# Router values in PSUM, one-column norms by partition scalars, and another engine order in both routers of an MoE-attention-MoE block

## The reference

```python
x = L0_attn_x                                        # 2048 tokens x 512
x = x + 0.5 * ffn(layernorm(x), router_w, w1, w2, w3)   # 8 experts, top 2
x = x + attention(layernorm(x), wq, wk, wv, wo)         # 16 query heads, 4 kv heads, rope, causal
x = x + 0.5 * ffn(layernorm(x), router_w, w1, w2, w3)   # the same weights

def ffn(x, ...):
    logits = x @ router_w.T                          # 8 columns
    topk_vals, topk_idx = top_k(logits, 2)
    w = softmax(topk_vals)
    out = sum_k w_k * (silu(x @ w1[e_k]) * (x @ w2[e_k])) @ w3[e_k]
```

## Time and profile before

| | |
|---|---|
| median of 3 runs | 1417.6 us (1414.39 to 1419.07) |
| profiled execution | 1419.23 us, its span 1417.9 |
| PE busy | 1220.3 us (86%) |
| DVE busy | 917.7 us (65%) |
| ACT busy | 662.2 us (47%) |
| POOL busy | 549.6 us (39%) |
| mean granted TensorE clock | 0.951 of full speed |

### The profile page before, as it was taken

One profiled execution on the slowest core, in us unless ns is written; L12 is line 12 of the kernel. 1 busy time (PEld: TensorE's weight loads), 2 busy tenths in 40 slices (PEclk: granted clock), 3 DMA queues, 4 the chain that ended last, 5 costly groups with the idle time before them and its releaser, 6 DMA issues.

```text
span 1417.9 us, 22075 instructions
## 1 busy us (share of the span) xinstructions
PE 1220.3 (86%) x7484; PEld 784.6 (55%) x7484; DVE 917.7 (65%) x2072; ACT 662.2 (47%) x1313; POOL 549.6 (39%) x458
## 2 busy tenths in 40 slices
PE   4279999948988999999989999999999538998884
PEld 3268888727776554454445455454433226766663
DVE  7777777668996565576676675767700785665653
ACT  2525545515455454454365554555566323444442
POOL 5535544323210110013353454445647443444442
PEclk8589999979999999999999999999999859999998
DMA  9713333256541022041013003013000343555544
GB/s 340 280 53 105 112 108 109 82 161 101 88 85 32 2 62 31 17 105 31 32 60 61 2 2 119 30 62 61 1 2 1 129 178 68 89 90 91 93 87 65
DMA packets 56891, 114.42 MB, mean 81 GB/s; under 512 B 7664, under 2 KB 17136, under 8 KB 56752
## 3 DMA queue, kind: packets, MB, share of 16 engines
q0 software_dynamic: 26112, 68.17, 22.0%
q1 hardware_dynamic: 30672, 44.85, 9.5%
HBM read 79.71 MB, written 33.55 MB: 80 GB/s over the span
## 4 chain that ended last, share of the span: by engine, by line
PE 58%; DMA 17%; DVE 16%; issue 4%; ACT 4%; SPq 1%; POOL 0%; POOLq 0%; DVEq 0%; ACTq 0%
DMA out<-Y,DI 12%; PE bank L1448 9%; PE bank L1460 9%; PE bank L752 9%; PE bank L907 8%; PE bank L1473 5%; PE bank L775 4%; PE bank L1510 3%; DVE PM L920 3%; DMA XA<-y 2%; DVE bank L922 2%; PE bank L734 1%; ACT P L1552 1%; PE bank L365 1%; PE bank L1490 1%
## 5 line engine op out<-in xcount | busy, mean ns | idle before, releaser
L1552 ACT ACTIVATE P<-bank 128x512 f32<-128x512 f32 (+3 forms) x640 | 305.5, 536 | 296.5 <-PE bank L1448 292.8
L920 DVE TENSOR_REDUCE PM<-bank 128x1 f32<-128x512 f32 x384 | 252.6, 685 | 99.2 <-PE bank L907 98.0
L1448 PE MATMUL bank<-Qs,Ks 98*128 98x512 f32 (+3 forms) x640 | 247.9, 412 | 7.9 <-ACT P L1552 6.3
L907 PE MATMUL bank<-Ks,Qs 96*128 96x512 f32 (+3 forms) x640 | 238.4, 391 | 9.6 <-DVE PM L920 5.0
L1448 PEld LDWEIGHTS bank<-Qs,Ks 98*128 98x128 f32 x640 | 117.3, 190 | 149.8 <-issue 84.7
L1606 POOL TENSOR_TENSOR CH<-CH,P 128x512 f32<-128x512 f32 x128 | 160.2, 1285 | 70.2 <-ACT P L1552 69.3
L922 DVE CUSTOM_DVE_ANT_0 bank<-bank,KB 128x128 f32<-128x128 f32 (+3 forms) x256 | 124.6, 496 | 57.4 <-PE bank L907 56.6
L1591 POOL TENSOR_SCALAR_AFFINE_SELECT P<-P 128x512 f32<-128x512 f32 x64 | 40.8, 638 | 308.3 <-ACT P L1552 308.3
L907 PEld LDWEIGHTS bank<-Ks,Qs 96*128 96x128 f32 x640 | 121.4, 190 | 64.0 <-DVE PM L920 32.6
L1460 PE MATMUL bank<-P,V 128*32 128x512 f32 (+3 forms) x1280 | 150.8, 542 | 0.2 <-POOL P L1591 0.2
L863 DVE TENSOR_TENSOR DL<-W,DH 128x512 fp32r<-128x512 f32 x152 | 98.3, 688 | 46.7 <-ACT DH L824 36.2
(11 more groups left out here) (176 smaller groups left out, 1936.9 us busy)
## 6 DMA issues: line engine op xcount, KB each, us to landing
xn<-XN SPq DMA_DIRECT2D x8, 1024.0 KB, 6.0
WR<-L_ffn_w POOLq DMA_DIRECT2D x16, 512.0 KB, 13.2
XO<-y POOLq DMA_DIRECT2D x8, 1024.0 KB, 9.5
WR<-L_ffn_w SPq DMA_DIRECT2D x16, 512.0 KB, 7.9
XA<-y POOLq DMA_DIRECT2D x24, 256.0 KB, 4.2
W<-L_ffn_w POOLq DMA_DIRECT2D x8, 512.0 KB, 24.2
XA<-L_attn_x SPq DMA_DIRECT2D x16, 256.0 KB, 3.5
XO<-L_attn_x SPq DMA_DIRECT2D x4, 1024.0 KB, 7.8
```

The costliest lines, as they stand in the source:

```text
L907: pe.matmul(bk(g, bank)[:, 0:n], g.Qs[b][0:96, G % 4 * 4 + h, c * P:c * P + P], g.Ks[0:96, G % 4, k * BQ:k * BQ + n], start=True, stop=Tru ...
L920: dve.tensor_reduce(dst, bk(g, bank)[:, 0:n], AX.X, ALU.max).then_inc(s(f"free{bank}"), 1)
L1448: pe.matmul(bk(g, i % 3)[:, o:BQ], g.Ks[0:98, G % 4, k * P:k * P + P], g.Qs[G // 4][0:98, G % 4 * 4 + j, o:BQ], start=True, stop=True).the ...
L1552: act.activation(a.P4[buffer_of(n)][:, j, o:BQ], bk(g, i % 3)[:, o:BQ], ACT.Exp, scale=scale).then_inc(s("exp"), 1)
```

## The change

It does five things. (1) Most intermediate values of `dve_route` are put into banks 6 and 7 (`route_banks`), so that an instruction has at most one input tensor in SBUF; a few copies are added for it (`M1`, a second half of `OH`, `tok`). (2) The Newton step of a single column takes its factors as partition scalars and has one instruction fewer (router 1's last quarter, and the 16 norms of the projection, L1119). (3) Router 0 turns two quarters ahead: the order of PE and of the banks is `first_order`, eight tiles of `xT` are held, the logits have a tile of their own, DVE handles the logits of quarter q-2 inside quarter q, and ACT makes one cast before its last four turns. (4) The tail of the plan has three of the steps `split1` before the norms and one behind each norm, the eighth behind the last turn, and the casts and subtractions behind the router are gone. (5) `TK` is made first from the slots, `DW` and `DI` behind it, and POOL waits for `TK` before it gathers and for `DI` before it writes.

The waits between the instructions are left out here:

```diff
 def router_memory(f, area, small, nx):
-    R.xT = area(f"xT{f}", [P, 4, D])
+    R.xT = area(f"xT{f}", [P, R.nt, D])          # R.nt = 4 * nx
+    R.lg = R.xT[:, 0, 0:P] if f else small("lg", [P, P])[:]
...
+def route_banks(g):
+    ps = Box()
+    a, b = bk(g, 6), bk(g, 7)
+    ps.OH = a[:, 0:256].rearrange("p (k i e) -> p k i e", k=2, e=NE)
+    ps.HF = a[:, 256:320].rearrange("p (h n) -> p h n", h=2)
+    ps.HI = a[:, 320:384].bitcast(I32).rearrange("p (h n) -> p h n", h=2)
+    ps.WV = a[:, 384:416].rearrange("p (h n) -> p h n", h=2)
+    ps.tok = a[:, 416:448]
+    ps.IF = a[:, 448:480].rearrange("p (k i) -> p k i", k=2)
+    ps.SF = a[:, 480:512]
+    ps.we, ps.M1, ps.tl, ps.en, ps.EF = ...      # bank 7
...
+def dve_newton_of_one(g, var, sd, y, t):
+    dve, dv = g.nc.vector, g.dv
+    dve.reciprocal(y, sd).then_inc(dv.sem, 1)
+    dve.tensor_scalar(t, y, y, var, ALU.mult, ALU.mult).then_inc(dv.sem, 1)
+    dve.tensor_scalar(t, t, -0.5, 1.5, ALU.mult, ALU.add).then_inc(dv.sem, 1)
+    dve.tensor_scalar(y, y, t, None, ALU.mult).then_inc(dv.sem, 1)
...
+def first_order():
+    def turns(q):
+        return [("turn", 0, 4 * q + c) for c in range(4)]
+    order = turns(0) + turns(1)
+    for q in range(4):
+        order += [("logits", 0, q), ("best", 0, q)] + (turns(q + 2) if q < 2 else [])
+    return order
...
 def act_first(g):
     act.wait_ge(s("xn0"), NT)
-    for e in range(4):
+    act_high(g, 0, 0)
+    for i in range(NT - 4, NT):
+        act_turn(g, R, i)
+    for e in range(1, 4):
         act_high(g, 0, e)
...
 def dve_first(g):
+        dve_variance(g, R, 0, 4, q)
+        if q >= 2:
+            dve_logits(g, R, q - 2)
+        dve_solve(g, R, 0, 4, q)
+        dve_room(g, R, q)
+        for c in range(4):
+            dve_scale(g, R, q, x4, c)
+        if q >= 2:
+            dve_best(g, R, q - 2)
+    for q in range(2, 4):
+        dve_logits(g, R, q)
+        dve_best(g, R, q)
...
 def dve_route(g, f, R, low_in_between):
-    dve.tensor_tensor(r.wd[:, 0, :], M8[:, :, 1], M8[:, :, 0], ALU.subtract).then_inc(rt.sem, 1)
+    dve.tensor_scalar(ps.M1, M8[:, :, 1], 1.0, None, ALU.mult).then_inc(rt.sem, 1)
+    dve.tensor_tensor(r.wd[:, 0, :], ps.M1, M8[:, :, 0], ALU.subtract).then_inc(rt.sem, 1)
-    dve.tensor_copy(r.IF[:], I8[:, :, 0:2].rearrange("p i k -> p k i")).then_inc(rt.sem, 1)
+    dve.tensor_scalar(ps.IF, I8[:, :, 0:2].rearrange("p i k -> p k i"), 1.0, None, ALU.mult).then_inc(rt.sem, 1)
+    # ps.OH <- iota, ps.IF (256 columns); r.OH[:, 1] <- iota, ps.IF (128 columns); r.A <- ps.OH[0], r.OH[1]
-    dve.tensor_tensor(r.A[:], r.OH[:, 0, :, :], r.OH[:, 1, :, :], ALU.add).then_inc(rt.sem, 1)
+    dve.tensor_tensor(r.A[:], ps.OH[:, 0, :, :], r.OH[:, 1], ALU.add).then_inc(rt.sem, 1)
+    dve.tensor_scalar(ps.tok, K[:, C_TOK:C_TOK + 2 * NT], 1.0, None, ALU.mult)
...
     for k in range(2):
-        dve.tensor_tensor(r.OH[:, k], r.SL[:], r.OH[:, k], ALU.mult).then_inc(rt.sem, 1)
+        dve.tensor_tensor(r.OH[:, k], r.SL[:], ps.OH[:, k], ALU.mult).then_inc(rt.sem, 1)
...
-    dve.tensor_copy(r.TF[:], ps[:, 0:NJ])
-    dve.tensor_copy(r.DW[:], ps[:, NJ:2 * NJ])
+    # TD, then TI and TK straight from the bank; DW and DI behind TK
...
 def pool_experts(g, f, before_adding):
-    pool.wait_ge(s(f"route{f}"), g.routed[f]["DI"])
+    pool.wait_ge(s(f"route{f}"), g.routed[f]["TK"])
...
+        if j == 1:
+            pool.wait_ge(s(f"route{f}"), g.routed[f]["DI"])
...
 def attend_plan(g):
-    plan += [("weigh", len(TILES) - 1), ("out", 15), ("up1", 4), ("tsum", 15), ("even", 15)]
+    plan += [("weigh", len(TILES) - 1), ("out", 15), ("up1", 4), ("split1", 0), ("split1", 1), ("split1", 2), ("tsum", 15), ("even", 15)]
     for c in range(6):
...
-            plan.append(("split1", c))
-    plan += [("logits", 3), ("best", 3), ("store", 3)]
+            plan.append(("split1", 3 + c))
+    plan += [("split1", 7), ("logits", 3), ("best", 3), ("store", 3)]
...
 def build(nc, d, out):
-        for e in range(4, NE):
-            act_high(g, 1, e)
-        for e in range(4, NE - 1):
-            pool_low(g, 1, e)
```

More of the change, by code:

```diff
@@ L273, in dve_solve @@
         dv.up()
-    var, sd, y, t = (sm[:, j, c0:c1] for j in range(4))
     dve.wait_ge(dv.sem, dv.n)
-    dve.tensor_scalar(var, R.mv[:, c0:c1, 1], 1e-5, None, ALU.add).then_inc(s(f"var{R.f}"), 1)
-    dve.wait_ge(s(f"sd{R.f}"), k + 1)
-    dve_newton(g, var, sd, y, t)
+    dve.tensor_scalar(sm[:, 0, c0:c1], R.mv[:, c0:c1, 1], 1e-5, None, ALU.add).then_inc(s(f"var{R.f}"), 1)
+def dve_solve(g, R, c0, c1, k):
+    g.nc.vector.wait_ge(g.s(f"sd{R.f}"), k + 1)
+    newton = dve_newton_of_one if c1 == c0 + 1 else dve_newton
+    newton(g, *(R.sm[:, j, c0:c1] for j in range(4)))
 def dve_newton(g, var, sd, y, t):
@@ L347, in act_turn @@
     act.wait_ge(s(f"full{bank}"), use + 1)
-    if i >= 4:
-        b0, u0 = g.ring.where[("best", R.f, i // 4 - 1)]
+    if i >= R.nt:
+        b0, u0 = g.ring.where[("best" if R.f else "logits", R.f, (i - R.nt) // 4)]
         act.wait_ge(s(f"full{b0}"), u0 + 1)
-    act.copy(R.xT[:, i % 4, :], bk(g, bank)).then_inc(s(f"free{bank}"), 1)
+    act.copy(R.xT[:, i % R.nt, :], bk(g, bank)).then_inc(s(f"free{bank}"), 1)
 def pe_logits(g, R, q):
@@ L373, in dve_logits @@
     dve.wait_ge(s(f"full{bank}"), use + 1)
-    dve.tensor_copy(R.xT[:, 0, 0:P], bk(g, bank)[:, 0:P]).then_inc(s(f"free{bank}"), 1)
+    dve.tensor_copy(R.lg, bk(g, bank)[:, 0:P]).then_inc(s(f"free{bank}"), 1)
 def pe_best(g, R, q):
@@ L395, in dve_best @@
     ins.then_inc(s(f"free{bank}"), 1)
-def first_plan(g):
[L402 to L406, removed]
+def first_order():
[5 more added lines that the diff above has]
+    return order
+def first_plan(g):
+    for key in first_order():
+        g.ring.take(key)
 def sp_first(g):
@@ L439, in act_first @@
     s, act, R = g.s, g.nc.scalar, g.R0
-    for q in range(5):
-        if q < 4:
-            act_sqrt(g, R, 0, 4, q)
+    for q in range(4):
+        act_sqrt(g, R, 0, 4, q)
         if q:
@@ L446, in act_first @@
     act.wait_ge(s("xn0"), NT)
-    for e in range(4):
+    act_high(g, 0, 0)
+    for i in range(NT - 4, NT):
+        act_turn(g, R, i)
+    for e in range(1, 4):
         act_high(g, 0, e)
 def pe_first(g):
-    for q in range(4):
-        for i in range(4 * q, 4 * q + 4):
+    for kind, _, i in first_order():
+        if kind == "turn":
             pe_turn(g, g.R0, i)
-        pe_logits(g, g.R0, q)
-        pe_best(g, g.R0, q)
+        elif kind == "logits":
+            pe_logits(g, g.R0, i)
+        else:
+            pe_best(g, g.R0, i)
 def dve_first(g):
     s, dve, R = g.s, g.nc.vector, g.R0
[L461 to L476, removed]
+    for q in range(4):
+        x4 = g.X[:, 4 * q:4 * q + 4, :]
+        for c in range(4):
+            if q == 0:
+                dve.wait_ge(s(f"x0_{c}"), 16)
+            elif c == 0:
+                dve.wait_ge(s(f"x{q}"), 16)
+            dve_stats(g, R, x4, c)
+        dve_variance(g, R, 0, 4, q)
[3 more added lines that the diff above has]
+        dve_room(g, R, q)
+        for c in range(4):
+            dve_scale(g, R, q, x4, c)
[4 more added lines that the diff above has]
+        dve_best(g, R, q)
 ORDER = (tuple(range(NE)), (4, 5, 6, 7, 0, 1, 2, 3))
@@ L635, in dve_route @@
     else:
[L636 removed]
+        dve.tensor_scalar(r.TD[:], sl[:, 2 * NJ:3 * NJ], g.Kc[:, C_PAD + 1:C_PAD + 2], g.Kc[:, C_PAD:C_PAD + 1],
+                          ALU.mult, ALU.add)
+        dve.tensor_copy(r.TK[:], sl[:, 0:NJ]).then_inc(rt.sem, 1)
     out["TK"] = rt.up()
[L638 removed]
+    dve.wait_ge(rt.sem, rt.n)
+    dve.tensor_copy(r.DW[:], sl[:, NJ:2 * NJ])
+    dve.tensor_tensor(r.DI[:], r.TD[:], sl[:, 0:NJ], ALU.add).then_inc(rt.sem, 1)
     out["DI"] = rt.up()
@@ L643, in act_route @@
 def act_route(g, f):
-    s, act, r = g.s, g.nc.scalar, g.r[f]
+    s, act = g.s, g.nc.scalar
     act.wait_ge(s(f"route{f}"), g.routed[f]["wd"])
-    act.activation(r.wd[:, 1, :], r.wd[:, 0, :], ACT.Exp).then_inc(s(f"we{f}"), 1)
+    act.activation(g.r[f].wd[:, 1, :], g.r[f].wd[:, 0, :], ACT.Exp).then_inc(s(f"we{f}"), 1)
 def pe_route(g, f):
@@ L1623, in pool_attend @@
                            accum_op=ALU.add).then_inc(s("xoy"), 16)
-        elif step[0] == "split1":
+        elif step[0] == "split1" and step[1] < NE - 1:
             pool_low(g, 1, step[1])
@@ L1682, in dve_attend @@
         elif kind == "solve":
+            dve_variance(g, g.R1, 0, 4, step[1])
             dve_solve(g, g.R1, 0, 4, step[1])
```

104 lines of the change are left out of this document (50 added, 54 removed).

## The result

| | before | after |
|---|---|---|
| median | 1418.34 us (1414.39 to 1423.05, 4 runs) | 1381.27 us (1377.62 to 1382.4, 4 runs) |
| ratio, 95% interval | | 0.9733 (0.9698 to 0.9768) |
| span of the profiled execution | 1417.9 us | 1381.1 us |
| mean granted TensorE clock | 0.951 | 0.958 |
| DVE busy | 917.7 us | 884.9 us |

What follows compares the result with a forecast made beforehand. The chain ends 58% on TensorE, but DVE stretches in both routers, before the expert stages, move the end. 1419.2 - 19.0 (router 0) - 21.6 (router 1) = 1378.6, from the median 1377.0; forecast 1378 us, range 1367 to 1391.

Steps and rivals of the forecast that it cites:

- rival D: POOL isn't what holds the DVE steps; only the new order and TK gain, 1413 us; chance 0.03.
- Router 0, first part: Router 0 up to the last maximum: turning two quarters ahead brings it to 41.0 us, -4.8 (bounds -3.7 to -5.9).
- Tables of router 0: Small DVE steps after router 0's last maximum take 1.7 us where 17.0 stood: -15.3 us.
- L577's hold: Router 0: L577, still SBUF to SBUF, waits for POOL's seam at 48.1 us: +1.5 (bounds 0 and 4.5).
- TK: In each router POOL waits for TK instead of DI, behind two steps fewer: -0.4 us each.
- Norms and tables of router 1: Router 1: norms -9.4 us, with scales still held to POOL's seams, and tables -12.2 us, together -21.6.
- Rival A: The scale isn't held, or PE stays warmer: L313 and L577 slip by under POOL, 1372 us; chance 0.14.
- The shorter Newton: Newton step in router 1's norms and the projection's 16: dropped step offset by partition scalars, 0 us (projection bounds -1.5, +1).
- PSUM operands: Both routers: reading operands from PSUM costs nothing by the profile rows; the skill's table would add 3 us.
- Rival E: Both routers: instructions writing or broadcasting from PSUM are dear, so the kernel ends slower, 1448 us; chance 0.02.
- Rival B: Both routers: a PSUM destination does not free an instruction with an SBUF input, 1388 us; chance 0.10.
- Rival C: POOL's queue without gaps gives DVE no seam; all norms wait until 1135.5 us; 1402 us; chance 0.04.

Runs made afterwards that it cites:

- experiment 1: Kernel before with POOL's subtractions given to DVE, all boxes still in SBUF: 1395.34 us, ratio 0.9855 to before.
- experiment 6: Kernel after with POOL's wait ahead of its gathers put back from TK to DI: 1381.26 us, ratio 0.9741 to before.
- experiment 2: Kernel after with the contents of route_banks in SBUF instead of banks 6 and 7: 1392.35 us, ratio 0.9813 to before.
- experiment 7: Kernel after with POOL's subtractions in four pieces each, 1378.35 us; with the exponential's offset written to bank 7, 1379.43 us; with both, 1376.41 us.

## Why the prediction was right

The forecast was 1378, and 1381.3 and 1379.3 were measured. Its account of both routers holds, and what is missing at the end comes mostly from outside them. By its steps:

- **What bounds.** Right, and now shown: POOL's subtraction holds a DVE instruction with two SBUF inputs, or a tensor_scalar or cast from SBUF to SBUF, until it ends; one gets in at each seam. Not held under the burst are the statistics (L273, 0.69 us), a reduction (L607, 0.22) and a tensor_scalar of one column (L318, 0.15), all of them reading SBUF. Taking POOL's work away (experiment 1) refutes rival D without any change of operands.
- **Router 0, first part**, -4.8. From the start of the first quarter's scale to the last maximum it is 31.1 us (31.0 when run again: 9.19 to 40.1) instead of 36.3 (9.51 to 45.85): -5.3, inside the bounds. In the profiled execution the first scale started 1.0 us later, so that only 4.3 shows. Over all thirteen profiled executions this part is 30.6 to 32.3 us with the new order and 33.6 to 36.3 with the old, so a single pair can miss by some 2 us.
- **Tables of router 0**, -15.3: 17.0 became 1.5, so -15.5.
- **L577's hold**, +1.5: it is L628's 3.08 us, to 50.1. The mechanism was right, the size too small: 2.9 us more than the 0.17 of the step itself. In the second execution the burst starts at 34.62 and the seam comes at 48.11, as forecast (34.5 and 48.1), but DVE is there at 45.49 and not at 46.6, since the last maximum comes at 40.1: +2.5. In the first, DVE is there at 47.01, but the burst starts 2 us later than forecast, at 36.57 behind ACT's cast (34.59 to 36.49), which waits for the last scale. The bounds (0 to 4.5) held both.
- **TK**, -0.4: too small in router 0, where the gather itself is also 1.8 us shorter (experiment 6).
- Router 0 in sum: -19.0 forecast, -18.5 at the first expert matmul.
- **Norms and tables of router 1**, -21.6: -21.3 measured between the same events. The norms (copy of SM to the end of the last scale) give 9.4 of it, as forecast. The ends of the scales, forecast 4.5 apart, are 4.7 apart. Rival A (L313 slips by) is refuted. It would have given 14.1 in the norms instead of 9.4; with shorter pieces some 3 us of that can be had. The tables' 12.2 are cured twice over: the boxes are in PSUM, and the burst is over (1120.51) when L604 starts. So in the kernel after, boxes in SBUF cost router 1 only 3.6 us (55.1 from the copy of SM to the second gather in experiment 2, for 51.5).
- **The shorter Newton**, 0 as arithmetic: right, since the step with two scalars costs 0.11 us more than a product did, the one with one scalar 0.05, and the dropped step saved 0.19. What it brings is the change of operands, 11 to 14 us in the final kernel, which the forecast has inside its term for the norms.
- **PSUM operands**, 0: right. From the groups by line and shape of the kernel after, 256 and 128 columns that touch a bank,

```profile
L588 DVE TENSOR_TENSOR bank<-KF,bank 128x256 f32<-128x256 f32 x2 | 0.9, 429 | 0.1
L602 DVE TENSOR_REDUCE bank<-cm 128x8 f32<-128x128 f32 x2 | 0.6, 295 | 0.1
```

and of the kernel without POOL's subtractions, the same from and to SBUF,

```profile
L539 DVE TENSOR_TENSOR OH<-KF,IF 128x256 f32<-128x256 f32 x2 | 0.9, 426 | 0.1
L549 DVE TENSOR_REDUCE tl<-cm 128x8 f32<-128x128 f32 x2 | 0.6, 286 | 0.1
```

  3 and 9 ns apart. L602 changes the destination alone. With the source alone in a bank, L620 (a cast of 32 columns) takes 192 ns against 182 for L569 of before, and L664 (39 columns) 199 against 183; the largest difference is L625, bank to bank, 232 against 194. The 62 cycles that the Trainium skill ("VectorE: DVE Perf Modes", on the TRN2 errata) puts between an SBUF and a PSUM source do not appear: the measurement decides against it. Rival E needed 580 ns on each and is refuted.
- **Rival B** (a bank as destination frees nothing) is refuted by L585 in the kernel after, and by L629 against L628 in experiment 7, where the destination alone was changed: 3.08 (2.66) to 0.17 us. The Trainium skill ("SBUF — State Buffer", "Who interferes with whom") speaks of a tensor_scalar from SBUF to SBUF; the trace agrees, 1.7 us for L341 under the burst against 0.55 outside it. **Rival C** is refuted by the seams.

Against the profiled execution the sum was -40.6 (1419.2 to 1378.6), and the spans differ by -36.8. Of the 3.8 us that are missing, router 0 has 0.5, router 1 0.3, the second expert stage 0.1, and the stretch between the routers 2.9. The sum held nothing for that stretch but the 16 norms, at 0 (bounds -1.5 and +1), and the norms are not what grew. By the prediction's own sign (an expert or attention stage that changes by over 2 us) something there was wrong: the runs show the lower clock in more of it, and leave the cause open. The first gathers came at 65.05 and 1137.39 us, where about 63 and 1134 were forecast, the second 36.9 us earlier instead of 41, mostly because of that stretch. In the routers the total was met term by term, and not by luck; in the stretch between, two executions of one kernel differ by more than the whole error (826.7 and 831.6).

## What to carry to other kernels

When a small DVE instruction takes microseconds, look at what POOL runs at that moment, and compare the end of the one with the end of the other. If they coincide, move the small values into a spare PSUM bank (as an input where there are two, as the destination of a copy or a tensor_scalar), before moving work from one engine to another. What has to stay from SBUF to SBUF under the burst is best helped by a shorter holder: four pieces of 512 columns lengthened the burst by 9% and cut a hold from 3 us to 0.45. Parts that cure the same wait need not add: measure each alone and each left out, and give both numbers. Here only the boxes were measured both ways (24 us alone, 11 left out); the Newton step and the two orders were only left out.

## What the runs showed of the hardware that was not expected

- The destination alone decides for a tensor_scalar of 16 columns: 3.08 us to SBUF, 0.17 us to a bank, under the same burst of POOL.
- A scalar operand read from a partition has a price: 0.15 us with constants, 0.21 with one, 0.27 with two (one column).
- Holding costs the holder little: seven subtractions with four scales in their seams took 32.16 us, 4.59 each, against 4.49 (8.98 / 2).
- The holding works both ways: a gather issued 0.35 us into a subtraction of DVE takes 2.82 us and ends 1.0 us behind the seam; issued 0.03 us into it, it takes 1.03.
- The first quarter's scale started between 9.11 and 10.85 us in the thirteen profiled executions, with the landing of X, although none of these kernels differs up to there. Within the routers, stretches between two events of one execution are steadier (22.5 and 23.5 us, 51.5 and 52.0, for the same kernel twice); the long one between them isn't (826.7 and 831.6).
